# One operand of VectorE's wide multiply moved to PSUM, the spread group split in halves, and GpSimd's step waits taken out

## The reference, cut to what matters

```python
z0   = einsum('bid,bjd->bdij', x0, x0)                    # 39 x 39 products
cur0 = relu(z0 @ W0)                                      # 128 outputs per (b, d)
next_h, direct0 = split(cur0, 2)                          # 64 and 64
z1   = einsum('bid,bjd->bdij', x0, next_h)                # 39 x 64 products
cur1 = relu(z1 @ W1)                                      # 128 outputs per (b, d)
z    = sum over d of concat(direct0, cur1)                # 192 features
y    = relu(relu(concat(z, dense) @ W_top1 + b1) @ W_top2 + b2) @ W_top3
```

## Time and profile before

| | |
|---|---|
| median of 3 runs | 420.97 us (420.96 to 422.31) |
| the profiled execution | 419.61 us, of which 417.8 us are its span |
| TensorE matmul busy | 395.1 us, 95% of the span, 1426 records |
| VectorE busy | 346.2 us, 83% |
| ScalarE busy | 227.4 us, 54% |
| GpSimd busy | 268.9 us, 64% |
| mean granted clock | 0.988 of full speed |

### The profile page before, as it was taken

One profiled execution on the slowest core, in us unless ns is written; L12 is line 12 of the kernel. 1 busy time (PEld: TensorE's weight loads), 2 busy tenths in 40 slices (PEclk: granted clock), 3 DMA queues, 4 the chain that ended last, 5 costly groups with the idle time before them and its releaser, 6 DMA issues.

```text
span 417.8 us, 4084 instructions
## 1 busy us (share of the span) xinstructions
PE 395.1 (95%) x1426; PEld 248.6 (60%) x1426; DVE 346.2 (83%) x198; ACT 227.4 (54%) x228; POOL 268.9 (64%) x164
## 2 busy tenths in 40 slices
PE   0797999799999999999999999999999999999997
PEld 0644655476565656665656666665656665656655
DVE  0127769697999999999998999999999999979940
ACT  1343476353847566574746564748466574745332
POOL 5778889888888888888888888888886000000000
PEclk9999799989999999999999999999999999999999
DMA  7158969496787869696969697898969595999200
GB/s 285 34 131 233 223 160 254 118 256 158 224 222 230 219 185 257 176 259 174 249 165 260 146 269 188 228 229 197 234 190 272 168 267 143 221 219 231 63 0 0
DMA packets 27862, 80.80 MB, mean 193 GB/s; under 512 B 7265, under 2 KB 16225, under 8 KB 20034
## 3 DMA queue, kind: packets, MB, share of 16 engines
q1 hardware_dynamic: 22354, 78.43, 71.7%
q0 software_dynamic: 5120, 1.32, 3.0%
q10 hardware_dynamic: 368, 0.80, 0.5%
HBM read 76.58 MB, written 3.93 MB: 193 GB/s over the span
## 4 chain that ended last, share of the span: by engine, by line
PE 63%; POOL 16%; DMA 9%; issue 7%; DVE 4%; ACT 1%; SPq 0%; ACTq 0%; DVEq 0%
POOL found L301 16%; PE acc L562 12%; PE acc L589 10%; PE acc L588 10%; PE acc L596 10%; PE acc L607 7%; PE sums L530 5%; DMA x_parts<-x_rows 3%; PE acc L603 3%; DMA found<-in_table_dram,rows_sb 3%; DMA x_rows<-found 3%; PE spread L640 2%; DVE z L447 2%; DVE z_lo L455 2%; PE spread L575 1%
## 5 line engine op out<-in xcount | busy, mean ns | idle before, releaser
L301 POOL DMA_INDIRECT found<-in_table_dram,rows_sb x160 | 268.7, 1679 | 51.3 <-issue 47.9
L455 DVE TENSOR_TENSOR z_lo<-z,z_hi 128x2048 fp32r<-128x2048 f32 x64 | 146.2, 2285 | 14.6 <-ACT z_hi L353 14.6
L353 ACT ACTIVATE z_hi<-z 128x2048 fp32r<-128x2048 f32 x63 | 120.3, 1910 | 67.0 <-DVE z L447 67.0
L447 DVE TENSOR_TENSOR z<-x_wide,h 128x2048 f32<-128x2048 f32 x64 | 145.1, 2284 | 3.3 <-DMA x_wide<-x_rows 3.3
L588 PE MATMUL acc<-z_hi,w_hi 128*128 128x512 f32 x256 | 108.1, 422 | 0.3 <-ACT z_hi L386 0.3
L562 PE MATMUL acc<-squares,w 128*128 128x512 f32 (+1 forms) x210 | 102.6, 606 | 0.0
L589 PE MATMUL acc<-z_hi,w_lo 128*128 128x512 f32 x256 | 101.1, 395 | 0.0
L596 PE MATMUL acc<-z_lo,w_hi 128*128 128x512 f32 x256 | 82.8, 446 | 0.8 <-DVE z_lo L455 0.8
L320 ACT ACTIVATE squares<-sums 128x1024 f32<-128x1024 f32 (+1 forms) x60 | 54.9, 914 | 46.0 <-PE sums L530 26.1
L596 PEld LDWEIGHTS acc<-z_lo,w_hi 128*128 128x128 f32 x256 | 48.6, 191 | 24.4 <-issue 14.9
L588 PEld LDWEIGHTS acc<-z_hi,w_hi 128*128 128x128 f32 x256 | 48.5, 189 | 15.8 <-issue 5.4
(11 more groups left out here) (60 smaller groups left out, 160.4 us busy)
## 6 DMA issues: line engine op xcount, KB each, us to landing
x_wide<-x_rows SPq DMA_DIRECT2D x64, 512.0 KB, 9.0
x_wide<-x_rows SPq DMA_DIRECT2D x112, 256.0 KB, 11.0
x_parts<-x_rows SPq DMA_DIRECT2D x31, 128.0 KB, 2.6
x_rows<-found SPq DMA_DIRECT2D x16, 240.0 KB, 2.5
x_wide<-x_rows SPq DMA_DIRECT2D x16, 192.0 KB, 6.9
found<-in_table_dram,rows_sb POOLq DMA_INDIRECT x160, 7.5
w_sb<-in_w_dram SPq DMA_DIRECT2D x1, 1280.0 KB, 8.5
x_wide<-x_rows SPq DMA_DIRECT2D x16, 64.0 KB, 6.5
```

What stands on the lines that cost most here:

```text
L301: pool.indirect_dma_start(out=found[:, b, 2, s * D:s * D + D], out_offset=None, in_=table, in_offset=bass.IndirectOffsetOnAxis(ap=rows_sb[ ...
L353: nc.scalar.activation(z_hi[:, n % RING], z[:, n % RING], ACT.Copy).then_inc(hi_done, 1)
L447: nc.vector.tensor_tensor(z[:, n % RING], x, h[:, c % 2, :].unsqueeze(1).to_broadcast([P, QUADS, N]), ALU.mult).then_inc(multiplied, 1)
L455: nc.vector.tensor_tensor(z_lo[:, n % RING], z[:, n % RING], z_hi[:, n % RING], ALU.subtract).then_inc(lo_done, 1)
```

## The change

The edits are these:

1. ScalarE evicts `acc0` twice more, into a new PSUM tensor `h_wide` of two banks (one for each parity of the chunk). The multiplies of groups 1 to 4 take `h_wide` in place of `h`. They are the ones that read `x_wide` from SBUF.
2. To make room, `spread` has two banks in place of four. Group 0 is spread and multiplied in two halves of two tiles. TensorE spreads the first half where it spread all four, and the second half inside `contract1_hi` of group 3, between its second and third tile, after VectorE has multiplied the first half.
3. VectorE multiplies the first half, then runs `reduce0`, then multiplies the second half. Chunk 0's second half goes into `sums`, behind the last W0 matmul, and the next `add_up` waits for its multiply.
4. SyncE waits for both `x_parts` transfers of chunk 1 before it issues the last two `x_wide` groups of chunk 0.
5. The table `in_step` and its waits on GpSimd are gone.
6. At the end, the second layer and y use `h_wide` banks where they used `spread` banks 2 and 3.

```diff
-        spread = ps("spread", [P, QUADS, N])
+        spread = ps("spread", [P, QUADS // 2, N])
+        h_wide = ps("h_wide", [P, 2, N])
...
             place(sp, 1, 0)
             place(sp, 1, 1)
+
+            sp.wait_ge(placed[1], 32)
             widen(0, 2)
...
-            in_step = {(1, 4): (w0_ready, 2), (1, 7): (summed, 2), (1, 8): (squared, 2), (1, 9): (squared, 3),
...
-                    if (c, s) in in_step:
-                        pool.wait_ge(*in_step[c, s])
...
                 nc.scalar.activation(h[HALF:P, par, :], acc0[0:HALF, :], ACT.Relu, scale=0.5).then_inc(h_ready, 1)
+                nc.scalar.activation(h_wide[0:HALF, par, :], acc0[0:HALF, :], ACT.Relu, scale=0.5).then_inc(h_wide_ready, 1)
+                nc.scalar.activation(h_wide[HALF:P, par, :], acc0[0:HALF, :], ACT.Relu, scale=0.5).then_inc(h_wide_ready, 1)
...
+                if half is not None:
+                    tiles = slice(2 * half, 2 * half + 2)
+                    dve.wait_ge(spread_done, 2 * c + half + 1)
+
+                    x = sums[:, :, :] if c == 0 and half else spread[:, :, :]
...
+                by = h_wide if half is None else h
+                nc.vector.tensor_tensor(z[:, n % RING, tiles, :], x,
+                                        by[:, c % 2, :].unsqueeze(1).to_broadcast([P, tiles.stop - tiles.start, N]),
+                                        ALU.mult).then_inc(half_multiplied if half == 0 else multiplied, 1)
...
-                    if g == G - 1 and 0 < c < CHUNKS - 1:
+                    if g < G - 1:
+                        multiply(n + 1)
+                    elif c + 1 < CHUNKS:
+                        multiply(n + 1, 0)
                         reduce0(c + 1)
-                    if n + 1 < G * CHUNKS:
-                        multiply(n + 1)
-                    if n == G - 1:
-                        reduce0(1)
+                        multiply(n + 1, 1)
...
+            def spread_out(c, half):
+
+                if c == 0 and half:
+                    pe.wait_ge(squared, T0)
+                elif half:
+                    pe.wait_ge(half_multiplied, c + 1)
                 elif c:
-                    pe.wait_ge(multiplied, G * (c - 1) + SPREAD[-1] + 1)
-                for q in range(QUADS):
+                    pe.wait_ge(multiplied, G * (c - 1) + 1)
+                for a in range(2):
+                    q = 2 * half + a
                     rows = slice(32 * q, 32 * q + 32)
...
+                    if g == G - 2 and a == 2 and n // G + 1 < CHUNKS:
+                        spread_out(n // G + 1, 1)
```

More of the change, by code:

```diff
@@ L146, in build @@
         hid1_acc = [sums[:, 0, :], sums[:, 1, :], acc0[:, :], spread[:, 0, :]]
-        hid2_acc = [spread[:, 1 + m, :] for m in range(M2 // P)]
-        y_acc = spread[0:1, 3, :]
+        hid2_acc = [spread[:, 1, :], h_wide[:, 0, :]]
+        y_acc = h_wide[0:1, 1, :]
         early, late = slice(0, B - 2 * CB), slice(B - 2 * CB, B)
@@ L431, in split, with multiply @@
                                         ALU.subtract).then_inc(found_lo_done, 1)
-            def multiply(n):
+            def multiply(n, half=None):
                 c, g = n // G, n % G
@@ L436, in multiply @@
                     dve.wait_ge(h_ready, 2 * (c + 1))
-                if g in SPREAD:
-                    dve.wait_ge(spread_done, len(SPREAD) * c + SPREAD.index(g) + 1)
-                    x = spread[:, :, :]
+                if g == 1:
+                    dve.wait_ge(h_wide_ready, 2 * (c + 1))
+                if half is not None:
+                    tiles = slice(2 * half, 2 * half + 2)
+                    dve.wait_ge(spread_done, 2 * c + half + 1)
+                    x = sums[:, :, :] if c == 0 and half else spread[:, :, :]
                 else:
+                    tiles = slice(0, QUADS)
                     dve.wait_ge(wide_in[WIDE.index(g)], 16 * (4 if g == WHOLE else 3) * (c + 1))
@@ L490, in _ @@
             split(1)
-            dve.wait_ge(h_ready, 2)
-            dve.wait_ge(spread_done, 1)
-            nc.vector.tensor_tensor(z[:, 0, 0:2], spread[:, 0:2, :],
-                                    h[:, 0, :].unsqueeze(1).to_broadcast([P, 2, N]), ALU.mult).then_inc(half_multiplied, 1)
-            nc.vector.tensor_tensor(z[:, 0, 2:], spread[:, 2:, :],
-                                    h[:, 0, :].unsqueeze(1).to_broadcast([P, 2, N]), ALU.mult).then_inc(multiplied, 1)
+            multiply(0, 0)
+            multiply(0, 1)
             for c in range(CHUNKS):
@@ L564, in contract0 @@
                 last.then_inc(contracted0, len(DUOS[d]))
-            def spread_out(n):
-                c, i = n // G, SPREAD.index(n % G)
-                if i:
-                    pe.wait_ge(multiplied, G * c + SPREAD[i - 1] + 1)
+            def spread_out(c, half):
[3 more added lines that the diff above has]
+                    pe.wait_ge(half_multiplied, c + 1)
                 elif c:
-                    pe.wait_ge(multiplied, G * (c - 1) + SPREAD[-1] + 1)
-                for q in range(QUADS):
+                    pe.wait_ge(multiplied, G * (c - 1) + 1)
+                for a in range(2):
+                    q = 2 * half + a
                     rows = slice(32 * q, 32 * q + 32)
-                    last = nc.tensor.matmul(spread[:, q, :], select_sb[rows, T0 + i, :], x_parts[rows, c % BUFS, :],
+                    to = sums[:, a, :] if c == 0 and half else spread[:, a, :]
+                    last = nc.tensor.matmul(to, select_sb[rows, T0, :], x_parts[rows, c % BUFS, :],
                                             start=True, stop=True)
@@ L671, in _ @@
             contract1_hi(0)
+            pe.wait_ge(multiplied, 1)
             add_up(ND)
@@ L696, in _ @@
                         contract0(2 * ND)
-                    if (n + 2) % G in SPREAD and n + 2 < G * CHUNKS:
-                        spread_out(n + 2)
+                    if g == G - 2 and c + 1 < CHUNKS:
+                        spread_out(c + 1, 0)
                     if g < 2 and c + 1 < CHUNKS:
```

14 lines of the change are left out of this document (5 added, 9 removed).

## The result

The changed kernel takes 425.38 us (median of 4 runs, 423.96 to 426.50), the kernel before 420.97 us beside it (4 runs). The ratio is 1.0106, with a 95% interval of 1.0055 to 1.0158: slower, by 4.4 us where 5.8 were forecast, and so by less than 2% but clear of no change. The profiled execution took 424.73 us, its span 422.9.

A forecast was written before the change was run, and what follows sets the result against it. TensorE alone was taken to bound the kernel; blocks +9.6, steady, first and last waits +0.6, +0.5, +0.7, gathers -4.7, chunk 0 -0.5, rare waits -0.4 gave +5.8 on 420.97: 426.8 us, range 420.5 to 432.

The forecast's parts named there:

- 15 blocks: TensorE, chunks 1 to 15: each added half-spread block costs 0.64 us for entering, streaming and leaving, +9.6 us in all.
- gathers, chunks 2 and 3: h in PSUM frees GpSimd, so late gathers stop delaying ScalarE and TensorE: -4.7 of 5.2 us lost in chunks 1 to 3.
- start, chunks 0 and 1: TensorE gains 0.5 us in chunk 0 from earlier `x_parts`; the second half's wait there costs about 0.5 us.
- steady wait and rare waits: TensorE's wait for the first half's multiply, +0.6 us in 14 chunks; rare later waits for `x_parts` go, -0.4 us.
- last boundary: At the last chunk boundary TensorE's second spread waits for late VectorE: 1.4 us less 0.78 already waited, +0.7 us.
- The lower bound, 0.23 for streaming: Lowest price of an added TensorE block, if its matmuls simply flowed: 0.23 us each, 3.5 us in all.
- the second half's first wait: In chunk 0 no `sums` pair stands between the halves, so TensorE waits about 0.5 us for VectorE's first multiply.
- What is late next is TensorE's own work: Once the waits for late gathers are gone, only TensorE's own work limits those chunks; 4.7 of 5.2 us comes back.
- The rival in which the fill wins: Chunk 0 wins all 5.4 us beside 5.2 in chunks 1 to 3; 418.4 us with blocks at 0.44; chance 0.13.
- The second half's wait: TensorE's second spread waits for VectorE's first multiply, fitting by a hair: 0.04 us a chunk, bounds 0 and 0.2.
- The rare waits: TensorE's rare waits for `x_parts` in later chunks, 0.4 us in all, should go as its chunks get longer.
- The waits of `in_step` cost nothing: GpSimd's idle time ahead of a gather is 0.30 us with or without such a wait, so removing them gains nothing.

The follow-up runs named there:

- both looks at the kernel before: The kernel before, unchanged, profiled first beside the change (420.97 us) and again on another chip (422.87 us).
- the moved spread alone: The kernel before with the four spread matmuls directly behind the 64-row pair of group 2: 421.11 us against 423.44, ratio 0.9921.
- the block alone: The kernel before with the spread issued as two pairs into their own banks, h still in SBUF, no new wait: 426.02 us, ratio 1.0167.
- the waits put back: The changed kernel with the table `in_step` and its waits on GpSimd restored: 428.21 us, ratio 1.0197.
- the fill-only kernel: The kernel before with h in PSUM and halves in chunks 0 to 2 only, no step waits: 447.99 us; with step waits added, 419.24 us.

## Why the prediction was right, and where it wasn't

The verdict, slower by about 1%, was right, and so was the term that made it. That the sum came within 0.7 us is in part luck, since the misses of the smaller terms cancel. What each term measured, by the table above:

| term | forecast | measured |
|---|---|---|
| 15 blocks | +9.6 | +9.6 |
| gathers, chunks 2 and 3 | -4.7 | -4.8 (49.26 + 1.28 - 45.76) |
| start, chunks 0 and 1 | 0.0 | +0.7 (-0.41 - 2.71 + 4.46 - 0.64) |
| steady wait and rare waits | +0.2 | +0.4 |
| last boundary | +0.7 | -0.8 |
| sum | +5.8 | +5.1 |

**The block.** Priced from the chain as 0.44 + 0.20 us, it is 0.64 in the changed kernel and 0.64 by itself in the kernel before. The lower bound, 0.23 for streaming, was far off. Two 128-row matmuls, with no change of mode, took 0.46 us in the first block and left nothing on the `sums` behind it: the excess of 0.20 does come with the 32-row matmuls.

**The gathers.** The size is right, and the cause that was given for it isn't the one that decides. That GpSimd is held up by the multiplies, and that h in PSUM frees it, is shown: chunk 3's gathers end at 58.01 us in the changed kernel and at 75.32 in the kernel before. But that the waits of the earlier trace rows go by this fell twice. They also go with h in SBUF and no step waits (22.88, 22.90), where chunk 3's gathers end at 66.51, and with h in SBUF and step waits once the chunks are a block longer (22.86, 22.90), where they end at 63.07 and the long gather falls on chunk 4. In the three other traces with h in SBUF and step waits (both looks at the kernel before, and the moved spread alone) it fell on the eighth or ninth gather of chunk 3. As far as these traces show, what decides is which gather, if any, comes to lie under VectorE's run of operations, and that shifts with each edit. The 46 us that GpSimd is spared (264.5 against 218.2) bought about 1 us in one trace (128.03 against 129.00) and nothing in the medians (425.38 against 425.27).

**Chunks 0 and 1.** Two errors that nearly cancel. Chunk 0 gained 2.71 us, not 0.5, since the slow clock of the earlier trace rows didn't come; without SyncE's wait it didn't come either, so that edit isn't its cause. An edit priced at nothing may be: three traces with step waits (the first, the block alone, the waits put back) have chunk 0 at 33.19 to 34.78 us and a clock of 0.50, 0.50 and 0.72 from 41 to 47 us, the three without them that didn't stall 31.30 to 31.83 us and a clock of 1.00. That is one trace each, so it isn't shown. Chunk 1 lost 3.82 us beside its block, where 0.5 was given for the second half's first wait. VectorE's 3.52 us for `x_wide` is the largest piece, and taking SyncE's wait away gives back 1.45. In the four kernels of the first chip the end of chunk 1 fell between 81.57 and 83.22 us. "What is late next is TensorE's own work" was wrong for chunk 1: it was `x_wide`. The rival in which the fill wins had its place right and its outcome wrong, because what chunk 0 won chunk 1 gave back.

**The second half's wait.** It fitted by a hair, as forecast: no wait in the steady chunks, where 0.04 us each was taken, and with 128-row spreads, a little earlier on TensorE, it began to bind. At the last boundary it waits 0.26 us, and 0.78 us of before are gone. The forecast carried 1.4 us over from VectorE's wait of 2.29 us for `x_wide`, and in the changed kernel VectorE has no such wait there.

**The rare waits.** The row of the table with +0.2 hides two misses: the steady wait is 0 in place of +0.6, and the rare longer chunks cost 0.4 us more than before in place of 0.4 less (23.75 and 22.99 us against 22.90, where the kernel before has 22.70 and 22.39 against 22.26). The waits for `x_parts` did not go as the chunks got longer: TensorE has one of 0.78 us in chunk 10, and with the step waits put back it is 3.01 us.

**The step waits.** "The waits of `in_step` cost nothing" holds in the first profile as far as GpSimd's idle time goes, although the gather at 62.07 that the prediction names has no step wait in the table. What they were for wasn't in it, nor in the prediction: it had no rival in which taking them out costs anything. On the first chip they bring nothing, and the first run of the change was of that kind. On the third, taking them out alone costs 26 us (447.40 against 421.19), and on the fourth the changed kernel takes 31 us more than it first did (456.07 against 425.38). The range of 420.5 to 432 holds for the first kind only, and that the first run was of that kind is luck too.

## What to carry to other kernels

Price an added matmul block by what the chain charges for it and for the instruction behind it, not by its streaming time. A freed engine is worth nothing until some wait ends on it, so ask of each stall what else would end it. And a wait that costs nothing in one trace may be holding something off: before such pacing is taken out, run the kernel without it on more than one chip.

## What the runs showed of the hardware

With GpSimd's gathers issued without a pause in chunk 0, the other engines were held up in four traces for most of the time that the gathers lasted; on the third chip the step waits alone made the difference (421.19 against 447.40 us). The records end each long wait of ScalarE about 2 to 4 us after GpSimd stops (53.18 and 55.15; 53.21 and 57.20). It isn't a full block: VectorE's copy got through at 32.01 us and the fill-only kernel's squares one by one (32.87, 50.37), with the gathers going on. In the kernel before with its step wait, where GpSimd paused 2.71 us, the copy came at 22.89. In the meantime VectorE and ScalarE stand still with their inputs ready, TensorE behind them, and the DMA engines are nearly idle. The view of the DMA queues between 25 and 55 us in the stalled run of the changed kernel, with packets, MB and share, is this:

```profile
q1 hardware_dynamic: 110, 0.55, 8.3%
q0 software_dynamic: 802, 0.21, 7.7%
```

In the undisturbed run the same stretch has these two kinds and also packets of the kind "instruction":

```profile
q1 hardware_dynamic: 1526, 5.75, 68.4%
q0 software_dynamic: 604, 0.16, 4.9%
q8 instruction: 1, 0.02, 0.2%
q14 instruction: 1, 0.01, 0.1%
```

The Trainium skill, "Runtime: NRT & Kernel Launch" (Instruction fetch mechanics), says that every engine fetches its code by DMA in blocks. That these fetches are what is held up isn't shown, since no such packet lies between 52 and 66 us either, where the stall ends. The cause stays open, and so does what sets the runs apart: the changed kernel ran twice and showed both, which a difference of the chip or of the moment could do. Within a run the executions were alike (454.62 to 459.49 us, and 423.96 to 426.50).

One change of TensorE's split fewer, of four a chunk, saved 0.2 us. And in chunk 0 a wait of TensorE of 2.38 us was followed by a granted clock of 0.50, the 1.2 GHz level, one of 1.90 us at the same place by 1.00, but one of 2.41 us by 1.00 too and one of 2.40 us by 0.72: the length of that wait alone doesn't decide it.
